# A new order of work at both ends of a cross-attention loop, and one output finished in two parts

## The reference

```
x = x + xattn(layernorm(x), ctx)
    # trans = ctx @ W.T + b ; p = softmax(q @ trans.T) ; relu((p @ ctx) @ W.T + b)
x = x + attn(layernorm(x))      # h = ln(.)*g1+beta1 ; q,k,v ; causal linear attention over batches ; wo ; gelu FFN
x = x + ffn(layernorm(x))       # mixture of 8 experts, top 2
```

## Time and profile before

| | |
|---|---|
| median of 3 executions | 689.59 us (688.12 to 691.75) |
| the profiled execution | 685.66 us, of which span 683.9 us |
| mean granted TensorE clock in it | 0.986 of full |
| PE busy | 641.6 us, 94% of the span |
| DVE, ACT, POOL busy | 423.7, 372.6, 254.6 us |
| PE idle, 0 to 236 us (prologue, loop, value products) | 8.2 us to the first matmul, then waits of 13.6 us |

### The profile page before, as it was taken

One profiled execution on the slowest core, in us unless ns is written; L12 is line 12 of the kernel. 1 busy time (PEld: TensorE's weight loads), 2 busy tenths in 40 slices (PEclk: granted clock), 3 DMA queues, 4 the chain that ended last, 5 costly groups with the idle time before them and its releaser, 6 DMA issues.

```text
span 683.9 us, 9655 instructions
## 1 busy us (share of the span) xinstructions
PE 641.6 (94%) x3418; PEld 532.7 (78%) x3419; DVE 423.7 (62%) x688; ACT 372.6 (54%) x523; POOL 254.6 (37%) x172
## 2 busy tenths in 40 slices
PE   5979998998998999989999999879999999999994
PEld 4868886886877788878888888677888888888883
DVE  7676667656777446576867444772674554763766
ACT  4599988987972254430143254311783645754760
POOL 5088886877884324341000050141022020220234
PEclk9999999999999999999999999979999999999999
DMA  9535453352141612222063891328598392991926
GB/s 321 202 124 192 144 181 132 129 173 84 35 140 52 194 62 92 85 101 63 1 239 131 319 342 61 124 77 293 182 365 311 96 333 69 353 374 50 348 81 184
DMA packets 51844, 116.95 MB, mean 171 GB/s; under 512 B 5208, under 2 KB 5208, under 8 KB 48736
## 3 DMA queue, kind: packets, MB, share of 16 engines
q1 hardware_dynamic: 47360, 106.51, 44.2%
q10 hardware_dynamic: 3168, 5.77, 2.5%
q0 software_dynamic: 1280, 4.20, 1.9%
HBM read 102.31 MB, written 14.16 MB: 170 GB/s over the span
## 4 chain that ended last, share of the span: by engine, by line
PE 80%; DVE 9%; issue 4%; ACT 3%; POOL 2%; DMA 1%; SPq 0%; DVEq 0%; ACTq 0%; POOLq 0%
PE bank L1351 19%; PE bank L1352 18%; PE bank L1353 18%; PE bank L1365 5%; PE bank L1416 3%; PE bank L1417 3%; PE bank L1384 3%; PE bank L1385 3%; PE bank L1758 1%; PE bank L1571 1%; POOL slots_x L529 1%; PE bank L1559 1%; PE bank L1401 1%; DVE xn L984 1%; PE bank L1745 1%
## 5 line engine op out<-in xcount | busy, mean ns | idle before, releaser
L468 POOL TENSOR_TENSOR nat_lo<-raw,nat_hi 128x512 fp32r<-128x512 f32 x104 | 134.3, 1314 | 48.6 <-ACT nat_hi L586 47.9
L517 POOL TENSOR_TENSOR e_lo<-e_raw,e_hi 128x2048 fp32r<-128x2048 f32 x9 | 41.6, 4621 | 221.6 <-ACT e_hi L743 221.6
L863 DVE TENSOR_TENSOR ct_lo<-bank,ct_hi 128x512 fp32r<-128x512 f32 x96 | 66.0, 689 | 43.7 <-ACT ct_hi L553 43.3
L1351 PE MATMUL bank<-w_hi,turned 128*128 128x512 f32 x176 | 70.7, 402 | 4.0 <-DVE turned L990 2.6
L1352 PE MATMUL bank<-w_lo,turned 128*128 128x512 f32 x176 | 69.4, 395 | 0.0
L1353 PE MATMUL bank<-w_hi,turned 128*128 128x512 f32 x176 | 69.4, 394 | 0.0
L553 ACT ACTIVATE ct_hi<-bank 128x512 fp32r<-128x512 f32 x96 | 57.0, 595 | 20.2 <-PE bank L1365 18.2
L586 ACT ACTIVATE nat_hi<-raw 128x512 fp32r<-128x512 f32 x104 | 64.9, 628 | 0.0
L1351 PE MATMUL bank<-e_hi,turned 128*128 128x512 f32 x144 | 59.0, 409 | 1.5 <-DVE turned L1279 1.5
L1365 PE MATMUL bank<-ident,raw 128*128 128x128 f32 x384 | 59.1, 278 | 0.0
L1365 PEld LDWEIGHTS bank<-ident,raw 128*128 128x128 f32 x384 | 48.2, 143 | 11.9 <-issue 0.2
(11 more groups left out here) (248 smaller groups left out, 1447.0 us busy)
## 6 DMA issues: line engine op xcount, KB each, us to landing
raw<-in_ctx_dram SPq DMA_DIRECT2D x24, 1024.0 KB, 5.1
w_raw<-in_L_ffn_w_dram SPq DMA_DIRECT2D x24, 1024.0 KB, 5.2
e_raw<-in_L_ffn_wo_dram SPq DMA_DIRECT2D x16, 1024.0 KB, 7.3
w_raw<-in_L_attn_w_dram SPq DMA_DIRECT2D x8, 1024.0 KB, 5.2
e_raw<-in_L_ffn_w_dram SPq DMA_DIRECT2D x8, 1024.0 KB, 7.4
slots_x<-zeros SPq DMA_DIRECT2D x1, 4096.0 KB, 15.9
slots_y<-zeros SPq DMA_DIRECT2D x1, 3840.0 KB, 25.3
vectors<-slots_x ACTq DMA_DIRECT2D x11, 256.0 KB, 4.2
```

Of the source, the lines that this page charges most:

```text
L468: nc.gpsimd.tensor_tensor(nat_lo[:, j, :], raw[b % 2][:, j, :], nat_hi[:, j, :].bitcast(f32), ALU.subtract).then_inc(nat_lo_ready, 1)
L517: nc.gpsimd.tensor_tensor(e_lo[j][:, :, :], e_raw[j][:, :, :], e_hi[j][:, :, :].bitcast(f32), ALU.subtract).then_inc(e_lo_ready[j], 1)
L863: nc.vector.tensor_tensor(ct_lo[:, n % CR, :], src, ct_hi[:, n % CR, :].bitcast(f32), ALU.subtract).then_inc(t_lo, 1)
L1351: nc.tensor.matmul(dst, lh, rh, start=first and k == 0, stop=False)
```

## The change

- **Prologue, DVE:** statistics, roots and `pn` of tiles 0 and 1 go ahead of those of tiles 2 and 3; DVE makes `W_lo` 0 to 2, POOL only 3, and only after all `pn`.
- **Prologue, PE:** the product for m = 0 stands directly behind the turned tokens, in three passes (hi x hi, lo x hi, hi x lo) with waits of their own; the first three context groups are turned after it. Before each of the products m = 1 to 3, and behind the last, one piece of `WT` is turned. All four pieces use bank 7. They are gone from steps 4, 6, 8 and 10 on all three engines.
- **ACT in the loop:** `pb` is copied at step 9. Value copies of batch 0 start at step 10; steps 18 and 19 have three each, and from step 20 the order is the old one.
- **Outputs:** `residual` is two functions. `output_taken` (`xo`, from the bank) stays at steps 54 and 80, `residual` (`xt`) is at steps 58 and 84, `first_stats` at 59 and 85. For output 2, `output_taken` stands directly behind the loop, ahead of the split of unit 0, and the rest behind `lower_turned(1)`.
- **Behind the loop:** units 1 and 2 are split by DVE instead of POOL. `sum_values` of the last batch stands between `lower_turned(0)` and `lower_turned(1)`. PE has `value_product(2)` ahead of `tile_turned(2)`.

```diff
+        def values_at(s):
+            if s < 18:
+                return range(s - 10, s - 9) if s >= 10 else range(0)
+            if s < 20:
+                return range(8, 11) if s == 18 else range(11, 14)
+            return range(s - 6, min(s - 5, B * NKT))
...
@@ POOL
-            for k in range(KD // 2, KD):
+            pool.wait_ge(pn_ready, NT)
+            for k in range(KD - 1, KD):
...
-            split_w(1)
             first_roots(3)
-            split_w(2)
...
@@ ACT, prologue and loop
+            upper_pw(0)
             for n in range(3):
                 upper_context(n)
...
+            for m in range(1, KD):
+                upper_WT(m - 1)
+                upper_pw(m)
+                upper_context(2 + m)
+            upper_WT(KD - 1)
...
-                if s in (4, 6, 8, 10):
-                    upper_WT(s // 2 - 2)
-                if s == 5:
+                if s == 9:
                     act.wait_ge(pb_done, 1)
...
-                if 0 <= s - 6 < B * NKT:
-                    upper_values((s - 6) // NKT, (s - 6) % NKT)
+                for i in values_at(s):
+                    upper_values(i // NKT, i % NKT)
...
@@ DVE, prologue
+            link(statistics((0, 1)))
+            variances(0)
+            last = statistics((2,))
+            tokens(0)
+            link(statistics((3,)))
+            variances(1)
+            lower_W(0)
+            lower_W(1)
+            tokens(1)
+            lower_W(2)
...
@@ DVE, loop
-                    if b % 2 == 1 and s == G * b + (41 if b < B - 3 else 45):
+                    if b % 2 == 1 and b < B - 3 and s == G * b + 41:
+                        output_taken(b // 2)
+                    if b % 2 == 1 and b < B - 3 and s == G * b + 45:
                         residual(b // 2)
+                    if b % 2 == 1 and b < B - 3 and s == G * b + 46:
                         dve.wait_ge(x1_ready, b // 2 + 1)
                         first_stats(b // 2)
...
@@ PE, prologue
+            pe.wait_ge(pnT_hi_ready, NT)
+            pe.wait_ge(pnT_lo_ready, 1)
+            for k in range(KD):
+                pe.wait_ge(W_hi_ready, k + 1)
+                nc.tensor.matmul(bank[3][:, :], W_hi[:, k, 0:P], pnT_hi[:, k, :], start=k == 0, stop=False)
...
+            for m in range(1, KD):
+                turned_W(m - 1)
+                token_product(m).then_inc(pwT_done, 1)
+                context_turned(2 + m)
+            turned_W(KD - 1)
```

More of the change, by code:

```diff
@@ L601, in upper_WT @@
                 act.wait_ge(WT_done, k + 1)
-                nc.scalar.activation(WT_hi[:, k, :], VB[k % 2][:, :], ACT.Copy).then_inc(WT_hi_ready, 1)
+                nc.scalar.activation(WT_hi[:, k, :], VB[1][:, :], ACT.Copy).then_inc(WT_hi_ready, 1)
             def upper_pw(m):
@@ L912, in lower_WT @@
                 dve.wait_ge(WT_hi_ready, k + 1)
[L913 removed]
+                nc.vector.tensor_tensor(WT_lo[:, k, :], VB[1][:, :], WT_hi[:, k, :].bitcast(f32), ALU.subtract).then_inc(WT_lo_ready, 1)
             def lower_pw(m):
@@ L925, in bias_part, with statistics, variances @@
                     last.then_inc(pb_done, 1)
-            for half in range(2):
-                for t in (2 * half, 2 * half + 1):
+            def statistics(tiles):
+                for t in tiles:
                     dve.wait_ge(x_loaded[t], 16)
                     last = nc.vector.bn_stats(stats[:, t, :], xt[:, t, :])
-                link(last)
+                return last
+            def variances(half):
                 for t in (2 * half, 2 * half + 1):
@@ L1435, in turned_W, with token_product @@
             def turned_W(k):
-                pe.wait_ge(pw_lo_ready, KD)
-                if k >= 2:
-                    pe.wait_ge(WT_lo_ready, k - 1)
+                if k >= 1:
+                    pe.wait_ge(WT_lo_ready, k)
                 for m in range(KD):
-                    mm = nc.tensor.transpose(VB[k % 2][:, m * P:(m + 1) * P], Wn[:, m, k * P:(k + 1) * P], ident[:, :])
+                    mm = nc.tensor.transpose(VB[1][:, m * P:(m + 1) * P], Wn[:, m, k * P:(k + 1) * P], ident[:, :])
                 mm.then_inc(WT_done, 1)
+            def token_product(m):
+                return product(bank[3 + m][:, :], [(W_hi[:, k, m * P:(m + 1) * P], W_lo[:, k, m * P:(m + 1) * P]) for k in range(KD)],
+                               [(pnT_hi[:, k, :], pnT_lo[:, k, :]) for k in range(KD)])
             pe.wait_ge(const_ready, 1)
@@ L1449, in _ @@
                 mm.then_inc(pnT_done, 1)
+            pe.wait_ge(pnT_hi_ready, NT)
[3 more added lines that the diff above has]
+                nc.tensor.matmul(bank[3][:, :], W_hi[:, k, 0:P], pnT_hi[:, k, :], start=k == 0, stop=False)
+            for k in range(KD):
+                pe.wait_ge(*((W_lo_ready, k + 1) if k < KD - 1 else (W_low_part, 1)))
+                nc.tensor.matmul(bank[3][:, :], W_lo[:, k, 0:P], pnT_hi[:, k, :], start=False, stop=False)
+            pe.wait_ge(pnT_lo_ready, NT)
+            for k in range(KD):
+                mm = nc.tensor.matmul(bank[3][:, :], W_hi[:, k, 0:P], pnT_lo[:, k, :], start=False, stop=k == KD - 1)
+            mm.then_inc(pwT_done, 1)
             for n in range(3):
                 context_turned(n)
-            for m in range(KD):
-                if m == 0:
-                    pe.wait_ge(pnT_lo_ready, NT)
-                for k in range(KD):
-                    if m == 0:
-                        pe.wait_ge(*((W_lo_ready, k + 1) if k < KD // 2 else (W_low_part, k + 1 - KD // 2)))
-                    mm = product(bank[3 + m][:, :], [(W_hi[:, k, m * P:(m + 1) * P], W_lo[:, k, m * P:(m + 1) * P])],
-                                 [(pnT_hi[:, k, :], pnT_lo[:, k, :])], k == 0, k == KD - 1)
-                mm.then_inc(pwT_done, 1)
-                if m < KD - 1:
-                    context_turned(3 + m)
+            for m in range(1, KD):
+                turned_W(m - 1)
+                token_product(m).then_inc(pwT_done, 1)
+                context_turned(2 + m)
+            turned_W(KD - 1)
             for s in range(NG_ALL):
@@ L1527, in _ @@
                 projected_out(NT - 1, k)
+            value_product(2)
             tile_turned(2)
-            for n in range(2, 5):
+            for n in range(3, 5):
                 value_product(n)
```

62 lines of the change are left out of this document (31 added, 31 removed).

## The result

The changed kernel takes 681.93 us, the median of 8 runs (681.34 to 682.66), against 689.0 for 8 runs of the kernel before (686.1 to 692.61). The ratio is 0.9896, with an interval of 0.987 to 0.9922: faster by 1.0%. The forecast was 679.0 with a range of its own from 676 to 682: the time lies inside it by 0.1 us.

A forecast was written before the change was run, and what follows sets the result against it. The prediction took PE as the bound: only holes in its stream and its clock count. Terms +2.4 -2.4 +0.5 -4.7 -1.7 -4.5 = -10.4 us took 685.66 to 675.3 profiled, median 679.0 us, own range 676 to 682.

The forecast's parts named there:

- 1, start: Prologue: first product 0.6 us sooner, context transposes behind it, lower PE clock after breaks; +2.4 us (0.6 to 3.2).
- 2, steps 0 to 13: Early loop: with eight ACT copies gone, the 2.77 us wait before step 13's scores shrinks; -2.4 us (-1.5 to -3.1).
- 3, copy burst: Steps 18 to 24: four more ACT value copies delay ct_lo and leave a small PE hole; +0.5 us (0 to 2.1).
- 4, outputs 0 and 1, with clock: Loop: two PE waits for pT shrink as DVE's residual work moves later; -4.7 us, plus -1.7 us of clock.
- 5, behind the loop: After the loop: smaller hole before value products, no clock drop, no wait at tile 3's turn; -4.5 us (-1.5 to -5.2).
- A hole of 0.6 to 0.7 stays: Before the scores of step 13: what remains of PE's 2.77 us wait after the change, in us.
- it can start some 0.3 us after the scores are done: Before step 13: ACT, rid of eight copies of about 0.5 us, can begin the third sc_low 0.3 us after the scores.
- so I allow 0.5: Behind the loop: 0.5 us allowed for DVE and POOL holding each other up; the 2.57 us hole shrinks by 1.9.
- Every later hole (expert layer, router) is untouched and should only move: After the changed stretch, up to 236 us: later PE holes only shift in time, with no gain or loss counted.
- With the same difference: Whole kernel: the median stays 3.9 us above the profiled execution, turning 675.3 into the forecast 679.0 us.

The follow-up runs named there:

- loop_end_only: Kernel before with only the changes behind the loop (output of tile 2 taken first, DVE splits, third value product earlier); median 687.13 us, ratio 0.9965.
- the kernel that had been warm: Changed kernel plus 24 identity transposes, result unread, on PE ahead of the first pn transposes; median 681.21 us, ratio 0.9893.

## Why the prediction was right, and where it was not

The direction and the places of the gain were right, and the time fell in the forecast's own range. That it did so is partly luck: two errors of several us partly cancel, and the time lies 0.1 us from the range's end.

| term | forecast | by the running difference |
|---|---|---|
| 1, start | +2.4 | +2.0 |
| 2, steps 0 to 13 | -2.4 | -1.15 |
| 3, copy burst | +0.5 | +0.7 |
| 4, outputs 0 and 1, with clock | -6.4 | -6.6 |
| 5, behind the loop | -4.5 | -3.2 |
| heads | 0 | +4.8 |
| rest | 0 | -0.4 |
| sum | -10.4 | -3.8 |

**1.** The loop's first turn starts at 30.04 in place of 26.24; 1.76 of the 3.8 are the four `WT` pieces (0.44 each) that moved there. The product began at 12.86, and its first two passes ran at the lower level until 16.4. That the breaks do this is shown by the kernels with and without them. What the step missed is that its base was one outcome of a draw: 13.84, from which it was counted, was the time of a start in which DVE was not held up.

**2.** "A hole of 0.6 to 0.7 stays": it was 1.18 before the scores of step 13, with two small ones ahead of it, 0.25 and 0.16. The step that failed is "it can start some 0.3 us after the scores are done": they were done at 40.95, and ACT, with context and value copies still ahead of it, began 1.0 later. The profile of before also hid a part of what this step is worth: five of the seven profiles with the wait of 2.77 lost 1.7 us of clock behind it, and none of the seven with the wait of 1.2 did. ACT in the changed kernel, and PE:

```profile
41.97 0.59 ACT L570 ACTIVATE sc_low<-bank 64x512 f32<-64x512 f32 x1
43.44 0.47 PE L1422 MATMUL bank<-ct_hi,pw_all 128*128 128x512 f32 x1 [1.18 <-DVE mx L881]
```

**3.** The burst was bounded rightly, 0.7 within 0 to 2.1.

**4.** Both holes closed for the stated cause, and alone this is most of the change. They gave 5.0, forecast 4.7; the step's own figures, 2 x (2.57 - 0.3) less 0.2, make 4.3. The other 1.6 are the clock's, forecast 1.7, and that part is luck of the profile of before: `loop_end_only` gained it with the hole open.

**5.** By the first value product the difference had grown by 1.4 (from -4.97 to -6.36), the hole's share, forecast 1.9. The turn of tile 3 gave 0.81 less a new wait of 0.28 for `av`, 0.5 in place of 0.9. What is left of the 3.2, 1.3, goes to the clock, forecast 1.7. The failed step is "so I allow 0.5": POOL's last piece, 1.29 us in before, took 3.87 over DVE's split of 2.27, and PE stood 1.06 us for it. The Trainium skill ("SBUF — State Buffer", Who interferes with whom) says that the two exclude each other for a whole instruction. The trace agrees, as 3.87 is more than 1.29 and 2.27 together. The prediction weighed this rule with DVE as the one that waits, for 0.8 us more than the 0.5; here it was POOL. The 5.07 us of the earlier trace rows became 0.87, as forecast.

**Heads.** The largest miss is "Every later hole (expert layer, router) is untouched and should only move". No term and no rival allowed for a fall of the clock at a hole that the change does not touch. That is 4.8 of the 6.6 us that the profile missed; 1.3 each are terms 2 and 5, less 0.8 elsewhere. Why all 8 runs of the changed kernel show a mean clock of 0.981 to 0.986, when the fall at one place comes in some kernels' profiles and not in others', stays open.

**The median.** "With the same difference" failed as well, the other way. Before, the median stood 3.9 us over the profiled execution; after, 0.1. That is mostly luck of the one profiled execution. In before, time and clock go together: of its 15 runs beside the first experiments the four at a mean clock of 0.991 took 682.8 to 685.1 us, the three at 0.977 took 691.6 to 692.5. The profiles show where: behind each of its four holes of about 2.5 us and more the clock may fall or not, for 0 to 3.4 us. The change closes two of them and brings the others to 1.2 and 1.1, and no profile shows a fall behind these. The changed kernel's 8 runs lie within 1.3 us, before's within 6.5. That the closed holes did this is not shown: the kernels with the filled start and with POOL's last piece on DVE, which have the same holes closed, spread over 5.1 and 3.4 us in six runs, with clocks up to 0.991, where the changed kernel's never exceed 0.986.

So the profile missed by 6.6 us one way and the median by 3.8 the other. The rest of the 2.9 by which the time was off is the 0.2 that 679.0 lies under the forecast's own sum: 689.59 - 10.4 is 679.2.

## What to carry to other kernels

A hole costs what PE stands, and on top a draw on the clock. Read the draw off several runs, not off the one profiled execution: closing a hole cannot give back more clock than falls behind it on average, and a hole that the change leaves alone can lose more than before. Work that nobody reads paid where nobody waits behind it: 2.1 us at the start by the timeline, 2.3 in the heads by the medians, though there the fall still came once in five profiles. Around the router it moved PE ahead and gained nothing, since PE's next input hangs on POOL's scatter. Where VectorE and GpSimd both subtract out of SBUF, put an order between them, and let the one go first for which PE waits: at the end of the loop that gave 1.2 us.

## What was not expected of the hardware

- The same wait of 1.42 us with the same work around it was followed by 0, 1.7, 3.4 or 6.8 us lost, in nine profiles; waits of 2.6 us by 0, 1.7 or 3.4.
- Near the router the loss was the same 5.1 us in eleven of fourteen profiles, whatever came before; the other three lost 3.4, 6.8 and 8.5.
- Two subtractions of DVE beside two of POOL took 1.28, 2.36 or 3.45 us, in the same stretch of five kernels.
- Until the level first rises a window shows 1.00, for the trace has no record of the clock before that: the first one is at 16.45 us in the changed kernel. There four matmuls of 512 columns took 1.88 us at 14.73, the spacing of the lower level, within this window:

```profile
12.00:16.00 4.00, 3.31 (x8) 2.48 (x8) 1.60 (x3) 0.60 (x1) 3.31 (x4) 1.00 1.02 419
```

In the kernel that had been warm the same four took 1.9 to 2.1, within this one:

```profile
12.00:18.00 6.00, 5.29 (x13) 4.02 (x14) 2.28 (x4) 0.66 (x2) 5.49 (x5) 0.50 1.03 406
```

At the start of a kernel the spacing has to be read, not the clock.
